# Block-local attention on one core: the scores computed a second time with the keys in rows, ten blocks later, in place of turning the probabilities

## The reference

```
q, k, v = layernorm(x) @ Wq.T, @ Wk.T, @ Wv.T              # 16 heads, D = 8
k2, v2  = [block n-1, block n] of k and of v               # 128 keys for 64 queries
scores  = einsum('bhnqd,bhnkd->bhnqk', qb, k2) * D**-0.5
scores  = where((j > i) & (j <= i + 64), scores, -1e30)
out     = einsum('bhnqk,bhnkd->bhnqd', softmax(scores), v2)
x       = x + out @ Wo.T
```

## Time and profile before

| | us |
|---|---|
| median of 3 runs | 2059.4 |
| lowest and highest | 2058.32 and 2070.29 |
| the profiled execution, its own time | 2058.17 |
| its span, first to last instruction | 2055.8 |
| TensorE busy | 1839.8 (89%) |
| VectorE busy | 1525.9 (74%) |
| ScalarE busy | 1237.9 (60%) |
| GpSimd busy | 1158.0 (56%) |

### The profile page before, as it was taken

How to read it: one execution, slowest core, us unless ns; L and a number is a source line. 1 busy time by engine, 2 the same in 40 slices (tenths; PEclk the granted TensorE clock), 3 DMA queues, 4 the chain that set the end, 5 groups by cost and what they waited for, 6 DMA issues and landing times.

```text
span 2055.8 us, 41241 instructions
## 1 busy us (share of the span) xinstructions
PE 1839.8 (89%) x15215; PEld 1330.3 (65%) x15215; DVE 1525.9 (74%) x3303; ACT 1237.9 (60%) x2837; POOL 1158.0 (56%) x878
## 2 busy tenths in 40 slices
PE   4769989899964989999999999999999999999949
PEld 3657777777744656666766766766766766766636
DVE  4667888888966668787777787777777788777553
ACT  5657777778734616556556566566566566555624
POOL 4100000000013818889779789789689788788855
PEclk8889999999977679999999999999999999999966
DMA  3635455456300000000000000000000000000002
GB/s 100 144 103 142 127 145 145 129 140 146 103 24 1 1 1 4 9 9 9 7 9 9 9 7 9 9 9 7 9 9 8 8 9 9 7 9 9 10 13 74
DMA packets 199243, 88.93 MB, mean 43 GB/s; under 512 B 149335, under 2 KB 174210, under 8 KB 198914
## 3 DMA queue, kind: packets, MB, share of 16 engines
q1 hardware_dynamic: 199042, 86.31, 18.4%
HBM read 39.83 MB, written 37.75 MB: 38 GB/s over the span
## 4 chain that ended last, share of the span: by engine, by line
PE 58%; DVE 22%; ACT 8%; issue 7%; POOL 4%; DMA 1%; SPq 0%; ACTq 0%; POOLq 0%; DVEq 0%
PE pair L1504 11%; PE pair L1408 9%; DVE amax L1416 7%; PE pair L1463 6%; PE pair L1459 6%; ACT prob L976 5%; DVE o_inv L1522 4%; PE pair L1211 3%; PE pair L1511 3%; ACT y L502 2%; PE pair L898 2%; DVE mx_neg L1019 2%; PE pair L1205 2%; DVE q_low L1350 2%; PE pair L788 2%
## 5 line engine op out<-in xcount | busy, mean ns | idle before, releaser
L1474 ACT ACTIVATE prob<-pair 128x512 f32<-128x512 f32 x1024 | 606.4, 598 | 466.7 <-PE pair L1463 409.7
L1416 DVE TENSOR_REDUCE amax<-pair 128x1 f32<-128x512 f32 x1024 | 663.6, 675 | 246.5 <-PE pair L1408 244.6
L1408 PE MATMUL pair<-key_hl,q_hi 128*128 128x512 f32 x1024 | 442.4, 435 | 28.0 <-DVE amax L1416 26.5
L1463 PE MATMUL pair<-q_low,key_h 65*128 65x512 f32 x1024 | 404.9, 395 | 0.0
L1459 PE MATMUL pair<-q_hi,key_hl 128*128 128x512 f32 x1024 | 404.2, 395 | 0.4 <-ACT prob L1474 0.4
L1488 POOL TENSOR_TENSOR Wm<-Wm,prob 128x1024 f32<-128x1024 f32 x160 | 381.5, 2384 | 27.4 <-ACT prob L1474 10.7
L1488 POOL TENSOR_TENSOR w_mix<-w_mix,prob 128x1024 f32<-128x1024 f32 x160 | 381.8, 2386 | 20.3 <-ACT prob L1474 2.8
L976 ACT ACTIVATE prob<-pair,mx_neg 128x128 f32<-128x128 f32 x1024 | 294.3, 388 | 116.5 <-DVE mx_neg L1019 109.2
L483 POOL TENSOR_SCALAR veps<-mv 128x8 f32<-128x8 f32 x48 | 11.5, 240 | 594.8 <-DVE mv L453 593.5
L1408 PEld LDWEIGHTS pair<-key_hl,q_hi 128*128 128x128 f32 x1024 | 196.3, 192 | 146.1 <-DVE amax L1416 55.3
L1504 PE MATMUL pair<-prob,values 128*32 128x256 f32 x4096 | 248.5, 383 | 0.0
(11 more groups left out here) (179 smaller groups left out, 2470.9 us busy)
## 6 DMA issues: line engine op xcount, KB each, us to landing
rows_mem<-once SPq DMA_DIRECT2D x256, 128.0 KB, 2.6
queries<-rows_mem SPq DMA_DIRECT2D x64, 256.0 KB, 4.9
keys<-rows_mem SPq DMA_DIRECT2D x16, 1024.0 KB, 5.4
q_low<-shift_cols SPq DMA_DIRECT2D x512, 0.5 KB, 2.0
yT<-o_norm SPq DMA_DIRECT2D x256, 32.0 KB, 1.8
x<-x_dram SPq DMA_DIRECT2D x8, 512.0 KB, 7.3
out_dram<-x SPq DMA_DIRECT2D x8, 512.0 KB, 3.2
Wm<-w_mla_dram SPq DMA_DIRECT2D x1, 1168.0 KB, 5.2
```

The source lines that it names most:

```text
L1408: e.matmul(bank(ROW_BANKS[n % 3]), q_hi[:, k, t * P:(t + 1) * P], key_hl[:, b % 2, i * HALF:(i + 1) * HALF], start=True, stop=True, skip_g ...
L1416: e.tensor_reduce(amax1[:, u % 2, t, i:i + 1], bank(ROW_BANKS[(2 * r + i) % 3]), AX_X, ALU.max).then_inc(*row_maxed.up((r, i)))
L1463: e.matmul(bank(j), key_h1[:, b % 2, ks], q_low[:, k, sl], start=False, stop=True, skip_group_check=True).then_inc(*key_scored.up((g, half)))
L1474: e.activation(prob1[:, g % P_BUFS, half * HALF:(half + 1) * HALF], bank(K_BANKS[(2 * g + half) % 3]), ACT.Exp, scale=SCALE1).then_inc(*ke ...
```

## The change

The scores of a block are still computed with queries in rows, and VectorE still takes their maxima, but nothing else is done with them: the two banks are free as soon as the maxima are taken. After eight steps TensorE turns the maxima of the half sequence (`pe_window_maxima`), ScalarE copies them to `mx_rows`, and four DMAs put them into one row of `queries` which meets a row of ones in `keys` (the remainder times remainder copy is given up for it: its rows are zeros, stored once by `sync_last_rows`). Ten steps after the first scores (`TURNED_LAG`) TensorE computes scores again with queries and keys exchanged (`pe_window_key_rows`), so that the keys are in rows and the negated maximum is already added. ScalarE takes one exponential of 512 columns per unit, straight into the tile that the weighing reads. The turning of probabilities and VectorE's copies of them are gone. Weighing starts 12 steps after the scores, and the plan has 143 steps instead of 135. `queries` has three buffers instead of two. SyncE issues both spreads before both gathers, and the maxima of the half sequence before behind them. GpSimd clears one buffer of queries at the very start of the program, and the other two after the sixth normalisation of stage a.

```diff
--- before.py
+++ after.py
@@ -130,6 +130,9 @@
 PAIRS = B * NB
+TURNED_LAG = 10
+WEIGH_LAG = TURNED_LAG + 2
+QUERY_BUFS = 3
...
@@ -154,7 +157,7 @@
         if kind == "v":
-            return n >= HB * (hb - 1) + 3
+            return n >= HB * hb + 3
...
@@ -404,13 +410,15 @@
-        S_BANKS, T_BANKS, O_BANK = (0, 1, 2), (3, 4), 5
+        S_BANKS, T_BANKS, MX_BANK, O_BANK = (0, 1), (2, 3), 4, 5
...
@@ -623,10 +631,11 @@
                 for b in range(3):
                     norm_pool(e, L, b, True)
-                pool_window_setup(e)
                 norm_pool(e, "w", 0, True)
                 for b in range(3, B):
                     norm_pool(e, L, b, True)
+                    if b == 5:
+                        pool_window_setup(e, False)
...
@@ -847,56 +857,102 @@
-                for again in range(2):
-                    e.dma_start(into[again], once[rows, i].bitcast(F32)).then_inc(bounced[i], 16)
+                e.dma_start(into[0], once[rows, i].bitcast(F32)).then_inc(bounced[i], 16)
+                e.dma_start(into[1, :, 0], once[rows, i, 0].bitcast(F32)).then_inc(bounced[i], 16)
...
+            e.wait_ge(*last_rows_stored)
             if i == 0:
-                e.wait_ge(*set_pool.at("slots"))
-                if hb >= 2:
-                    e.wait_ge(*scored.at(2 * HB * (hb - 1) - 1))
+                if hb < QUERY_BUFS:
+                    e.wait_ge(*set_pool.at(("slots", hb)))
+                else:
+                    e.wait_ge(*key_rows.at(2 * HB * (hb - QUERY_BUFS + 1) - 1))
...
+        def sync_last_rows(e):
+            e.wait_ge(*set_pool.at("last rows"))
+            for i in range(2):
+                for h in range(4):
+                    e.dma_start(rows_mem[i, h, REP - 1].rearrange("d q c -> (d q) c"),
+                                last_rows[:, i, :]).then_inc(last_rows_stored[0], 16)
+
+        def sync_move_maxima(e, hb):
+            e.wait_ge(*mx_copied.at(hb))
+            for r in range(2):
+                for s in range(2):
+                    row = (2 * r + s) * REP * D0 + (REP - 1) * D0
+                    e.dma_start(queries[row:row + 1, hb % QUERY_BUFS, :, :, s, :].bitcast(F32).rearrange(
+                        "o q m w -> o (q m) w"),
+                        mx_rows[r * QUADS * HB:(r + 1) * QUADS * HB, hb % 2, s * W:(s + 1) * W].bitcast(F32)).then_inc(
+                        mx_moved[hb % 2], 16)
 
         def pe_window(e):
...
             for n, items in enumerate(plan_w):
+                if n % HB == 0 and 0 <= n - HB < PAIRS:
+                    pe_window_maxima(e, n // HB - 1)
                 if n < PAIRS:
                     pe_window_scores(e, n)
-                if 0 <= 2 * n - 3 < units:
-                    pe_window_turn(e, 2 * n - 3)
+                if 0 <= n - TURNED_LAG < PAIRS:
+                    pe_window_key_rows(e, n - TURNED_LAG)
+                if n % 2 == 0 and 0 <= n - WEIGH_LAG < PAIRS:
+                    pe_window_weigh(e, (n - WEIGH_LAG) // 2)
+                if n % 2 == 1 and 0 <= n - WEIGH_LAG - 1 < PAIRS:
+                    pe_window_back(e, (n - WEIGH_LAG) // 2)
                 for slot in items:
                     if slot:
                         pe_window_part(e, *slot)
...
-        def pe_window_turn(e, u):
-            e.wait_ge(*exps.at(u))
-            if u >= 2:
-                e.wait_ge(*p_taken.at(u - 2))
+
+        def pe_window_maxima(e, hb):
+            e.wait_ge(*negated.at(2 * HB * hb + 2 * HB - 1))
+            if hb:
+                e.wait_ge(*mx_copied.at(hb - 1))
+            e.transpose(bank(MX_BANK)[0:2 * QUADS * HB, 0:P], mx_neg[:, hb % 2].rearrange("p r q m -> p (r q m)"),
+                        eye).then_inc(*mx_turned.up(hb))
+
+        def pe_window_key_rows(e, n):
+            hb, m = divmod(n, HB)
+            b, half = divmod(hb, 2)
+            k0 = W * (half * HB + m)
+            if m == 0:
+                e.wait_ge(mx_moved[hb % 2], 64 * (hb // 2 + 1))
+            if n:
+                e.wait_ge(*exps.at(2 * n - 1))
+            for r in range(2):
+                rows = slice(64 * r, 64 * r + 64)
+                e.matmul(bank(T_BANKS[r]).rearrange("p (q k) -> p q k", q=QUADS),
+                         mask_bf[rows, 1 if half == m == 0 else 0, :],
+                         both_rows[rows, :].unsqueeze(1).broadcast_to([W, QUADS, P]), start=True, stop=False,
+                         skip_group_check=True)
             for q in range(QUADS):
-                ins = e.transpose(bank(T_BANKS[u % 2])[:, q * P:(q + 1) * P], prob[:, u % 4, q, :], eye)
-            ins.then_inc(*p_turned.up(u))
+                for r in range(2):
+                    rows = slice(64 * r, 64 * r + 64)
+                    ins = e.matmul(bank(T_BANKS[r])[:, q * P:(q + 1) * P], keys[rows, b % 2, q, k0:k0 + 2 * W],
+                                   queries[rows, hb % QUERY_BUFS, q, m].rearrange("p s w -> p (s w)"), start=False,
+                                   stop=True, skip_group_check=True)
+                    if q == QUADS - 1:
+                        ins.then_inc(*key_rows.up(2 * n + r))
...
@@ -927,22 +983,21 @@
             if n:
-                e.wait_ge(*exps.at(2 * n - 2))
+                e.wait_ge(*negated.at(2 * n - 1))
...
@@ -969,13 +1032,11 @@
         def act_window_exponentials(e, u):
-            e.wait_ge(*negated.at(u))
-            if u >= 4:
-                e.wait_ge(*p_turned.at(u - 4))
-            for q in range(QUADS):
-                ins = e.activation(prob[:, u % 4, q, :], bank(S_BANKS[u % 3])[:, q * P:(q + 1) * P], ACT.Exp,
-                                   bias=mx_neg[:, u % 4, q:q + 1])
-            ins.then_inc(*exps.up(u))
+            e.wait_ge(*key_rows.at(u))
+            if u >= P_TURNED:
+                e.wait_ge(*weighed.at((u - P_TURNED) // 4))
+            e.activation(pT[:, u % P_TURNED].rearrange("p q k -> p (q k)"), bank(T_BANKS[u % 2]), ACT.Exp).then_inc(
+                *exps.up(u))
...
@@ -1005,18 +1062,13 @@
-        def dve_window_take(e, u):
-            e.wait_ge(*p_turned.at(u))
-            if u >= P_TURNED:
-                e.wait_ge(*weighed.at((u - P_TURNED) // 4))
-            e.tensor_copy(pT[:, u % P_TURNED].rearrange("p q k -> p (q k)"), bank(T_BANKS[u % 2])).then_inc(
-                *p_taken.up(u))
...
@@ -1035,12 +1087,17 @@
+        def pool_window_setup(e, early):
+            if early:
+                e.memset(last_rows[:, :, :], 0.0).then_inc(*set_pool.up("last rows zero"))
+                e.wait_ge(*set_pool.at("last rows zero"))
+                e.memset(last_rows[0:QUADS, 1, :], 1.0).then_inc(*set_pool.up("last rows"))
+                for i in range(2):
+                    e.memset(vals[:, i, :, :, VW - 1:VW], 1.0)
+                    e.memset(keys[:, i, :, 0:W].bitcast(F32), 0.0)
+            for k in range(1) if early else range(1, QUERY_BUFS):
+                e.memset(queries[:, k, :, :, :, :].bitcast(F32), 0.0).then_inc(*set_pool.up(("slots", k)))
...
@@ -1696,14 +1754,15 @@
-            for i in range(2):
-                sync_spread(e, 0, i)
-            for i in range(2):
-                sync_gather(e, 0, i)
-            for hb in range(1, 2 * B):
-                for i in range(2):
-                    sync_spread(e, hb, i)
-                    sync_gather(e, hb, i)
+            sync_last_rows(e)
+            for hb in range(2 * B + 1):
+                if hb < 2 * B:
+                    for i in range(2):
+                        sync_spread(e, hb, i)
+                    for i in range(2):
+                        sync_gather(e, hb, i)
+                if hb:
+                    sync_move_maxima(e, hb - 1)
```

100 lines of the change are left out of this document (50 added, 50 removed).

## The result

The changed kernel takes 1966.87 us (median of 4 runs, 1958.45 to 1968.4), the kernel before 2059.77 us (4 runs, 2058.32 to 2070.29): ratio 0.953, 95% interval 0.9489 to 0.9571, faster by 4.7%. The forecast was 1997 us and its range ended at 1965, so it had a gain of 62 us where 93 were measured, a third too little.

What follows compares the result with a forecast made beforehand. The prediction saw a ring of waits among TensorE, VectorE and ScalarE, with TensorE's own work close below. It summed 2058.2 - 51.7 - 25.5 + 18.5 - 4.0 = 1995.5 us, so 1997 as median, range 1965 to 2040.

Steps and rivals of the forecast that it cites:

- Term 1: The 111 steps from the seventeenth to the last scores: 3.33 us each, 369.6 against 421.3 us, so -51.7 us.
- (c): Steady steps: "once", ScalarE's copy and VectorE's subtraction delay the next maxima, 0.55 us lost four times in 16 steps, 2.2 us.
- (d): Steady steps: twice in 16 steps ScalarE scales four tiles, falls 1.5 us behind, and the rows of keys wait.
- (e): Steady steps: turning the maxima on TensorE, twice in 16 steps, 0.5 us.
- Term 2: The first 16 steps: lighter steps and earlier keys, step 16 at 46.7 us after step 0 instead of 72.2, -25.5 us.
- Ring (a): Scores wait for both VectorE maxima of the step before, 2.3 us; hidden by TensorE's work in steady steps.
- Term 3: The drain after the last scores: ten steps in 26 us, then last weighing and last step; 39 against 20.5, +18.5 us.
- ring (b): Rows of keys wait for both exponentials of the step before, 2.1 us; hidden in steady steps, 2.2 us in the drain.
- Term 4: Stage a: GpSimd's clearing no longer stands before the normalisation ScalarE waits for, -4 us, bounds -6 and +2.
- The bound by transfers: Rival, steady steps: slow transfers bound every half sequence, 29.7 us instead of 22, 42 us more, 2039 us; chance 0.1.
- The slower case: Rival, steady steps: ScalarE's exponentials find nothing beside them on TensorE, 4.46 us per step, 2122 us; chance 0.06.
- The case of an equal ring: Rival: steps don't get shorter, as another ring of the same length takes over, 3.64 us or more, 2031 us; chance 0.1.

Runs made afterwards that it cites:

- e10: Changed kernel with TensorE's part "out" moved from the step after a "once" to behind the next "once"; 111 steps 341.7 us against 342.0, total 1967.9 us.
- e2: Changed kernel with one more ScalarE copy of 398 columns at the end of each step; 111 steps 346.7 us against 342.0, total 1978.9 us.
- e1: Changed kernel with four more turning matmuls on TensorE in each step; 111 steps 390.8 us against 342.0, total 2014.8 us.
- e3: Changed kernel with one more VectorE pass over 398 columns between the two maxima of each step; 111 steps 356.9 us against 342.0, total 1982.4 us.
- e4: Changed kernel with SyncE's old order of spreads and gathers from the second half sequence on; 111 steps 354.5 us against 342.0, total 1975.5 us.
- e6: Changed kernel with key rows 9 steps after the first scores instead of 10, weighing still at 12; 111 steps 362.0 us against 342.0, total 2000.2 us.
- e5: Changed kernel with GpSimd's clearing, now three buffers, back in front of the normalisation ScalarE waits for; first scores at 86.4 us, total 1983.0 us.
- e7: Changed kernel without the mask matmuls in the first scores; 1966.28 us, ratio to the kernel before 0.9534.
- e9: Changed kernel without masks in the first scores and with ScalarE instead of SyncE issuing the maxima's four DMAs; 1986.7 us, ratio to the kernel before 0.9651.

## Why the prediction was too cautious

By its own terms, against the profiled execution:

| term | forecast | measured |
|---|---|---|
| 1, steady steps | -51.7 | -78.7 |
| 2, first 16 steps | -25.5 | -23.2 |
| 3, drain | +18.5 | +12.4 |
| 4, stage a | -4.0 | -5.3 |
| rest of the program | 0 | -4.7 |

**Term 1: the step that failed is the waits (c) and (d), put at 3.7 us in 16 steps.** The waits measured are 5.2 us over 111 steps, 3.7 for maxima and 1.5 for keys' DMA (which the sum had at nothing), so 0.75 us in 16 steps: (3.7 - 0.75) x 111 / 16 = 20 of the 27 us. TensorE's own work is the other part, and nearly right: 49.0 us and 0.5 for the turning of the maxima (e) were summed, and 342.6 - 5.2 = 337.4 us over 111 steps make 48.6, so 6 us in all; the first scores take 0.63 us from start to start, where 0.72 was taken from the earlier trace rows. Undisturbed, 16 steps take 49.1 us with 0.5 us of waits for maxima in them. The ring (c) was built rightly and over-priced, at 0.55 us four times where it is 0.27 twice. The excess is in durations added up that overlap, and in the small groups that stand between and take up a rest of 0.3 us (e10). ScalarE never held TensorE back at the scaling of tiles (d): the view of waits has no matmul that waits for an exponential in the 111 steps, and e2 gave ScalarE 0.53 us more per step for 4.7 us. So 3.09 us per step came out at the sum's lower bound (3.06), not at its middle (3.33). That the TensorE bound itself is right is shown by e1 together with e3.

**Term 2** was right in its mechanism and nearly in its size. Keys set both times: step 8 came at +21.9 us (21.2 forecast), step 16 at +49.0 (46.7), as their DMA took 6.9 us to land in both places, instead of the 5.5 taken from the earlier trace rows, and the second was issued 1.3 us later than forecast. In the chain that ended last they stand as:

```profile
89.62 6.88 DMA keys<-rows_mem
116.77 6.88 DMA keys<-rows_mem
```

The 5.5 us were read in the old order of issues, and the new order, which the term counts on, is what made the landing longer (e4: 5.4 us with the old order). All in all the new order is worth 4.6 of the 23.2 us. Ring (a) was put at 2.3 us in the first eight steps and was 2.73 at the low clock; it came within 1.1 us of setting step 8.

**Term 3** was too high in two of its three parts: ten steps took 22.3 us and not 26, and from the last weighing 8.1 and not 10.2. The step behind both is the clock: 0.78, the mean over the drain of before, was carried over to all of it. By parts, the drain of before up to the last weighing, and from there to the next stage, and then the latter in the changed kernel:

```profile
573.60:583.87 10.27, 5.88 (x74) 4.72 (x74) 8.72 (x30) 4.78 (x15) 1.24 (x2) 1.00 0.01 1
583.87:594.10 10.23, 6.99 (x56) 5.52 (x56) 3.71 (x13) 1.19 (x2) 0.66 (x1) 0.57 0.01 2
491.20:499.26 8.06, 4.81 (x57) 3.76 (x57) 1.59 (x5) 1.19 (x2) 0.00 (x0) 0.88 0.01 2
```

So the clock of before was 1.00 up to the last weighing, with TensorE busy for 57% of the time, and 0.57 behind it, after a wait of 3.62 us. In the changed kernel the wait ahead of the last weighing is 0.98 us, and the clock is 1.00 in the ten steps and 0.88 after them. The steps are ring (b), 2.0 us where no part stands, 2.1 forecast. The Trainium skill (TensorE: Matmul & The Clock Gate, Part 1: the default is throttled, activity releases it) was used for a drain at 1.2 GHz throughout, 29 us. That did not happen. A fall of the clock behind idle time is seen in e6, behind a wait of 2.74 us, in the two rows at 123.8 us above (after a wait of 3.5 us the scores take 1.33 us instead of 0.75), and in the first eight steps, with waits of about 1.4 us in each. Waits of up to 0.7 us, as the ten steps have, did not lower it.

**Term 4** was right: clearing in front of a normalisation for which ScalarE waits is paid in full (e5). Stage a has its own scatter, though, with first scores between 72.5 and 74.8 us in runs with the same stage a, so that 5.3 is known to some 2 us.

**The rivals.** The bound by transfers was not there, with 1.5 us of waits for keys in 111 steps. These waits grow to 4.4 us when TensorE has 1.6 us less in 16 steps (e7) and to 11.0 when the order of SyncE is turned back (e4). The slow issues in the price, 4.9 and 5.8 us, are the longest of their kinds in the profile of before; what made them slow no run shows. The slower case did not come; e9 shows what its mechanism takes here, a hold of ScalarE of 2.5 us in one piece, and costs, 17.5 us. The case of an equal ring is excluded by TensorE's 98% and by e3.
